# FFN 1 of a gated two-layer Flamingo block adds its rows in the output tensor itself; unused lanes are left to the transfer's bound

## What is computed

```python
_, idx = jax.lax.top_k(probs + gate_b, 6)
cw = einsum('tk,tke->te', take_along_axis(probs, idx), one_hot(idx, 16))
for e in range(16):            # a scan
    h = silu(xf @ W1[e].T + B1[e]) * (xf @ W3[e].T + B3[e])
    y = y + cw[:, e:e+1] * (h @ W2[e].T + B2[e])
z = silu(xf @ ws1.T + bs1) * (xf @ ws3.T + bs3) @ ws2.T + bs2
x = x + tanh(g_ffn[1]) * (y + z)     # this is the output
```

## Time and profile before

| | us |
|---|---|
| median of 3 runs | 2212.12 (2212.05 to 2216.62) |
| the profiled execution, whole | 2214.83 |
| its span | 2213.0 |
| PE busy in the span | 1899.8 (86%) |
| DVE busy | 1129.0 (51%) |
| ACT busy | 897.3 (41%) |
| POOL busy | 975.1 (44%) |

### The profile page before, as it was taken

One profiled execution on the slowest core, in us unless ns is written; L12 is line 12 of the kernel. 1 busy time (PEld: TensorE's weight loads), 2 busy tenths in 40 slices (PEclk: granted clock), 3 DMA queues, 4 the chain that ended last, 5 costly groups with the idle time before them and its releaser, 6 DMA issues. The chain is left out here.

```text
span 2213.0 us, 36441 instructions
## 1 busy us (share of the span) xinstructions
PE 1899.8 (86%) x10825; PEld 1562.9 (71%) x10825; DVE 1129.0 (51%) x2223; ACT 897.3 (41%) x1490; POOL 975.1 (44%) x704
## 2 busy tenths in 40 slices
PE   4568999969893679998788999999998799899995
PEld 2256778757771456665556777899997789899994
DVE  4834564423334697788845656444443334344442
ACT  5652222123343888988743132233332223233331
POOL 5353755625452778888600101243333333333331
PEclk8779999988995789998889999999999999999998
DMA  9376766898988675234621001946489894754444
GB/s 343 122 251 216 215 201 210 291 301 214 279 209 170 167 221 124 41 54 127 206 95 48 3 29 51 349 78 164 80 244 315 242 317 90 217 100 78 80 82 110
DMA packets 131458, 372.69 MB, mean 168 GB/s; under 512 B 20456, under 2 KB 24424, under 8 KB 126104
## 3 DMA queue, kind: packets, MB, share of 16 engines
q1 hardware_dynamic: 82616, 261.73, 37.2%
q0 software_dynamic: 33600, 79.73, 19.3%
q10 hardware_dynamic: 15072, 29.04, 3.6%
HBM read 209.93 MB, written 151.86 MB: 163 GB/s over the span
## 5 line engine op out<-in xcount | busy, mean ns | idle before, releaser
L1737 PE MATMUL ps<-f_wb,f_xThi 128*128 x2088 | 538.5, 340 | 27.6 <-issue 21.4
L1861 POOL DMA_INDIRECT y_scratch<-f_yo,f_rows x150 | 237.9, 1586 | 492.3 <-issue 274.1
L1737 PEld LDWEIGHTS ps<-f_wb,f_xThi 128*128 128x128 f32 x2088 | 372.3, 193 | 40.0 <-issue 31.3
L1737 PE MATMUL ps<-f_wb,f_xTlo 128*128 x1044 | 347.1, 332 | 0.0
L763 POOL TENSOR_TENSOR a_elo<-a_e,a_ehi 128x1024 f16<-128x1024 f32 x128 | 288.6, 2272 | 64.8 <-ACT a_ehi L856 62.5
L1756 PE MATMUL ps<-f_wb,f_hThi 128*128 (+2 forms) x822 | 278.7, 420 | 7.8 <-DVE f_hTlo L2136 7.8
L2154 DVE TENSOR_TENSOR f_g<-ps,f_bb 128x352 f32<-128x352 f32 x111 | 58.3, 525 | 341.2 <-PE ps L1737 338.4
L1834 POOL DMA_INDIRECT f_xg<-xn_scratch,f_rows x150 | 161.2, 1074 | 157.1 <-PE ps L1721 115.8
L1573 ACT ACTIVATE f_yo<-ps,f_share 128x512 f32<-128x512 f32 x150 | 103.2, 688 | 264.9 <-PE ps L1756 191.0
L1737 PEld LDWEIGHTS ps<-f_wb,f_xTlo 128*128 128x128 f32 x1044 | 201.1, 193 | 0.0
L1040 DVE TENSOR_REDUCE a_nmax<-ps 128x1 f32<-128x512 f32 x256 | 164.1, 682 | 43.0 <-PE ps L893 42.8
(11 more groups left out here) (251 smaller groups left out, 3602.6 us busy)
## 6 DMA issues: line engine op xcount, KB each, us to landing
f_wb<-w_scratch SPq DMA_DIRECT2D x16, 2816.0 KB
w_scratch<-f_stage_up SPq DMA_DIRECT2D x27, 1024.0 KB, 5.6
w_scratch<-a_stage_up SPq DMA_DIRECT2D x23, 1024.0 KB, 5.3
f_stage_raw<-in_f_w_dram SPq DMA_DIRECT2D x29, 768.0 KB
f_wb<-w_scratch SPq DMA_DIRECT2D x16, 1024.0 KB
w_scratch<-f_stage_down SPq DMA_DIRECT2D x108, 128.0 KB
f_wb<-w_scratch SPq DMA_DIRECT2D x8, 1536.0 KB
a_later_raw<-in_f_w_dram SPq DMA_DIRECT2D x16, 768.0 KB, 5.1
```

The source lines that it names most:

```text
L1737: mm = pe.matmul(out, xt[:, b % 2, k, :], weights(at, w, k, low), start=(m == 0), stop=(m == 3 * KD - 1))
L1861: pool.indirect_dma_start(y_d, bass.IndirectOffsetOnAxis(ap=rows_of[:, b:b + 1], axis=0), yo[:, b % 3, :], None, bounds_check=ROWS + SPARE ...
```

## The change

FFN 1's `y_d` is no longer a scratch tensor but the output tensor itself, seen as 2048 rows. So `keep` writes x into the output, and each block adds its rows there. The output has no spare rows: the scatter's bound is row 2047, a row number beyond it is not an error, and such a lane is left out. The four copies at the end, their count and SP's wait for them go. One of four zero fills at the start (FFN 1's y) goes, and SP awaits three. The gathers still read spare rows of the scratch `xn_d`. FFN 0 is as before.

```diff
-        y_d = [nc.dram_tensor(f"y{i}_scratch", (ROWS + SPARE, D), F32, kind="Internal").ap() for i in range(2)]
+        y_d = [nc.dram_tensor("y_scratch", (ROWS + SPARE, D), F32, kind="Internal").ap(),
+               a["out"].rearrange("b s d -> (b s) d")]
...
-                for i, m in enumerate(MOE):
-                    for to, width in ((g["xn_d"][i], D + m["E"]), (g["y_d"][i], D)):
-                        sp.dma_start(to[ROWS:ROWS + SPARE, :].rearrange("(r p) d -> p r d", p=P),
-                                     zero[:, 0:width].rearrange("p (o d) -> p o d", o=1).to_broadcast([P, 3, width])
-                                     ).then_inc(zero_out, 16)
+                for to, width in ((g["xn_d"][0], D + MOE[0]["E"]), (g["xn_d"][1], D + MOE[1]["E"]), (g["y_d"][0], D)):
+                    sp.dma_start(to[ROWS:ROWS + SPARE, :].rearrange("(r p) d -> p r d", p=P),
+                                 zero[:, 0:width].rearrange("p (o d) -> p o d", o=1).to_broadcast([P, 3, width])
+                                 ).then_inc(zero_out, 16)
...
-                sp.wait_ge(zero_out, 16 * 4)
+                sp.wait_ge(zero_out, 16 * 3)
...
-        out_done = sem("out_done")
...
+        LAST_ROW = ROWS + SPARE - 1 if layer == 0 else ROWS - 1
...
-                for t in range(B):
-                    if layer == 0:
+                if layer == 0:
+                    for t in range(B):
                         sp.dma_start(x[:, TB * t:TB * t + TB, :],
                                      y_d[S * t:S * t + S, :].rearrange("(t p) d -> p t d", p=P)
                                      ).then_inc(x_back[t], 16)
-                    else:
-                        sp.dma_start(a["out"][t, :, :], y_d[S * t:S * t + S, :]).then_inc(out_done, 16)
-                if layer == 1:
-                    sp.wait_ge(out_done, 16 * B)
...
                     pool.indirect_dma_start(y_d, bass.IndirectOffsetOnAxis(ap=rows_of[:, b:b + 1], axis=0),
-                                            yo[:, b % 3, :], None, bounds_check=ROWS + SPARE - 1,
+                                            yo[:, b % 3, :], None, bounds_check=LAST_ROW, oob_is_err=layer == 0,
                                             compute_op=ALU.add).then_inc(scattered[b % 3], 16)
```

## The result

The changed kernel takes 2189.47 us (median of 7 runs, 2185.24 to 2202.29) against 2212.12 us before (7 runs, 2205.84 to 2216.62). The ratio is 0.9913, with a 95% interval of 0.989 to 0.9935, so 14 to 24 us are gained. A second set of runs gave 0.9934 (0.9905 to 0.9964), 8 to 21 us. Single executions of the kernel before differ by up to 1.4% within a set, those of the changed one by 0.8%, so the sum of the parts is read better from the traces than from the times. The kernel before was timed beside each set of experiments, and its median was 2210.96 us for e1 to e4, 2206.23 for e5 to e8 and 2203.64 for e9 to e12. So medians are compared within a set only, and ratios are to the kernel before of the same set.

A forecast was written before the change was run, and what follows sets the result against it. TensorE was taken to bound most of the FFN blocks, with weight-fetch waits in places and a serial DMA tail. From the 2212.12 us median, -14.7 -2.0 -1.5 +0 = -18.2 gave 2193.9 us, range 2187.5 to 2201.5.

The forecast's parts named there:

- Part 1: End of the span: without the four output copies it ends 14.7 us earlier, with GpSimd's drain next.
- Part 2: FFN 1's last scatter carries no row, so its transfer time leaves the path: -2.0 us, bounds 0 and -2.9.
- Part 3: FFN 1's stretches waiting on weight fetches: less scatter traffic beside them gives -1.5 us, bounds 0 and -4.
- Part 4: Kernel start: one zero fill less brings the third weight chunk up to 2.0 us earlier; worth 0, bounds -2 and +2.
- (a): Scatters: lanes beyond the bound still run their packets, so only the copy is saved: 2197.4 us, chance 0.20.
- (b): End of the span: GpSimd's drain becomes the tail at 8.2 us, as in FFN 0: 2198.7 us, chance 0.12.
- (c): Kernel start: the shift meets VectorE badly, +9 us on the sum: 2202.9 us, chance 0.07.
- (d): GpSimd's generation: skipping lane by lane makes scatters long, slower than before; 2267 us at a 4.0 us scatter, chance 0.05.
- (e): Something unseen of 10 to 18 us, in output memory or fetch overlap, eats the gain: 2208 to 2216 us, chance 0.04.

The follow-up runs named there:

- e1: The kernel before, run again with no edit: 2211.46 us, ratio 1.0013.
- e4: The changed kernel with a fourth zero fill of 0.79 MB put back at the start, into scratch nobody reads: median 2191.14 us, ratio 0.9905.
- e5: The changed kernel, run again with no edit for a second trace: ratio 0.9934.
- e8: The changed kernel with 102 blocks in FFN 1 in place of 111: median 2140.69 us, ratio 0.9696.
- e9: The changed kernel with FFN 1's scatter bound at row 0, so nearly every lane is left out: median 2182.28 us, ratio 0.9902.
- e12: The changed kernel with one more, empty block in FFN 1 (112 blocks): 2197.8 us, one run.
- e2: The kernel before without FFN 1's four copies to the output and the wait for them: median 2195.61 us, ratio 0.9934.
- e3: The kernel before with only FFN 1's scatter bound at row 2047 and no error beyond; scratch and copies stay: median 2202.96 us, ratio 0.9971.
- e7: The changed kernel with FFN 1's very last scatter (block 110, no token) not issued: ratio 0.9936.
- e6: The kernel before with both the bound of row 2047 and the four copies out, rows still added in scratch: ratio 0.9914.
- e11: The changed kernel with FFN 1's last three scatters, of empty blocks, not issued: 2180.81 us, one run.

## Why the prediction was right, and where it was not

**Part 1, the copies: right, size and successor.** -14.7 foreseen, -14.8 in e2, with the drain next and 0.4 us behind, as the drain's end in rows 5 said.

**Part 2, the last scatter: the mechanism was right, its place on the path was not.** The rows' 2.0 us exist (3.2 to 1.2 us from generation to SP, here and in e3). The step that failed is "I take -2.0": it counted them on the path, though part 1 had just put the drain there. In its place the runs show -0.6 for the tail (9.16 in e2, 8.57 after). 0.1 of it is the drain, the rest is GpSimd's first load from its table behind the last yo. Queue instructions of that line, at the end of e2 and of the changed kernel (ns min/median/max):

```profile
L1852 POOLq TENSOR_LOAD <-f_table x2: 293/562/832, 2189.7 to 2190.7; - x2
```
```profile
L1852 POOLq TENSOR_LOAD <-f_table x2: 288/290/291, 2180.2 to 2180.7; - x2
```

The first of the two loads takes 0.83 us while the scatter before moves its rows, and 0.29 us where that one is empty. It took 0.83 to 0.91 us in the four traces where that scatter moved rows, and 0.29 in the other ten. The bound of 0 was nearer to the truth than the -2.0 that I took. The estimate of 0.6 us for moving the rows, worked out from the page of the Trainium skill ("DMA: Bandwidth & Descriptors", Anatomy of one DMA — SWDGE (gpsimd) path), is not borne out: the traces have 2.0 us. Its fixed part of some 2.0 us can't be set against one row here: an empty scatter landed 1.2 us after the end of its generation, 2.7 us after its start. That 0.6 us is also what the tail lost is chance.

**Part 3, the scatters under the fetches: right in mechanism, and in size as far as it can be told.** -1.5 foreseen; four fetches in a row are 2.0 us shorter, the stretch is 2.1 shorter in the mean (which could be scatter), and 1.9 is scaled from e9. How much of it reaches the end is not measured. The forecast that TensorE's waits for weights would be seen shorter was wrong: single traces differ by more than that. The wait for gathered rows, which e9 loses, had no term in the sum.

**Part 4, the fill: right at 0, by a wrong step.** That the third weight chunk would land up to 2 us earlier assumed that a transfer taken out lets all behind it move up. No such shift shows (e4).

**Rivals.** (a) is half true: the packets do run, 144 of them for an empty block, but they are empty: 2.4% of 3 us of the engines, against 53.8% of 4 us. The forecasts of 16 packets for an empty block and of some 1,920 fewer in all were wrong. The time alone would not have ruled (a) out: it forecast 2197.4, and the second set's ratio gives 2197.5. (b): the drain is the tail, as (b) said, but at 5.2 us and not FFN 0's 8.2; with 299 issued transfers in place of 300 it lasts 9.4 us (e7). (c): the hold of VectorE did not stay put as part 4 said: in the changed kernel it is another instruction and 11.9 us long, in e5 there is none. The start of FFN 1's blocks does not follow it. (d): the scatter's generation has a mean of 1586 ns against 1584, and the stretch bound by TensorE is unchanged. (e): nothing of 10 to 18 us is seen against the gain; e6 and the changed kernel, which differ in the memory behind y_d, end alike.

The sum by the parts as measured is -14.8 - 0.6 - 2.1 + 0 = -17.5 us, where the forecast had -18.2; that it comes so near owes something to luck, since part 2 was 1.4 us too large and part 3 some 0.6 too small. The two ratios to the kernel before are -19 and -15 us, one on either side of it. The median of the first runs, 2189.47, is 4.4 us below the forecast of 2193.9; the 4 us by which its profile reached the blocks early are of that kind, and belong to no part.

## What to carry to other kernels

When a tail of several waits is cut, put all of them in a row with their ends before counting: the second latest takes over, and a gain on the third is worth nothing. Here a copy at the end that only moved a result to its place was wholly on the path, and adding in the place itself took it out at no cost that the runs show. Empty lanes that a bound dropped still had their packets but not their bytes, which paid only where other transfers were waited for.

## What the runs showed of the hardware

An indirect scatter of 128 rows whose lanes are all out of bounds keeps its 144 packets and its 1.55 us of generation, but is seen landed by SP 1.2 us after it, against 3.1 to 3.2 us with rows. GpSimd's drain after indirect transfers lasted 3.5 to 7.6 us beyond the last generation. That went with how many had been issued (3.46 us behind 300, 7.62 behind 299), and by 0.2 us at most with what they moved. The 300th transfer, and the 192nd, started 1.3 us late in every kernel that had one. Rows scattered beside weight fetches lengthened four fetches from 66.4 to 73.8 us. A VectorE instruction on 4 elements a partition lasted 7.2 to 11.9 us at the start of thirteen of the fourteen traces, until near the end of a run of GpSimd's instructions, and 1.2 us in the remaining one:

```profile
21.33 11.90 DVE L115 TENSOR_TENSOR mdif<-mdif 128x4 f32<-128x4 f32 x1
```
```profile
21.17 1.24 DVE L115 TENSOR_TENSOR mdif<-mdif 128x4 f32<-128x4 f32 x1
```

These are the same instruction of the same kernel, in the changed kernel's first trace and in e5. It is a tensor_tensor; in before a tensor_scalar was hit. And executions of one kernel spread by 1.2% and more: 29 runs of the kernel before, on one chip, lay between 2194.66 and 2221.65 us, so differences under some 5 us had to be read from parts of the trace.

On these inputs e8 is faster than both kernels by far (2140.69 us, ratio 0.9696). e11 has a tail 8.3 us shorter than the changed kernel's, but its time is one run (2180.81 us, where the kernel before beside it had 2203.64). Both rest on the routing of these inputs; neither is a kernel for others.
